# Weighted values with the values as weights: two groups' outputs in one PSUM bank, copied, turned back and added together

## What is computed

```python
ln_lat = layer_norm(latents, g2, b2); q = ln_lat @ Wq
kv = concatenate([layer_norm(x, g1, b1), ln_lat], axis=1) @ Wkv
k, v = split(kv, 2, axis=-1)                       # then 16 heads of 64
weight = einsum('bhld,bhnd->bhln', q * scale, k * scale)
weight = softmax(where(full_mask, weight, -max))   # full_mask: the mask, and all latents
out = einsum('bhln,bhnd->bhld', weight, v)         # then @ Wout, added to the latents
```

## Time and profile before

| | us |
|---|---|
| median of 3 runs | 1055.75 (1055.22 to 1056.27) |
| the profiled execution | 1054.65 |
| its span, first to last instruction | 1052.8 |
| TensorE busy in the span | 1014.3 |
| VectorE, ScalarE, GpSimd busy | 809.3, 666.8, 204.1 |
| cross stage, 30 to 660 us: TensorE, VectorE, ScalarE busy | 622.99, 485.98, 385.82 |

### The profile page before, as it was taken

How to read it: one execution, slowest core, us unless ns; L and a number is a source line. 1 busy time by engine, 2 the same in 40 slices (tenths; PEclk the granted TensorE clock), 3 DMA queues, 4 the chain that set the end, 5 groups by cost and what they waited for, 6 DMA issues and landing times. The chain is left out here.

```text
span 1052.8 us, 25657 instructions
## 1 busy us (share of the span) xinstructions
PE 1014.3 (96%) x8683; PEld 943.1 (90%) x8684; DVE 809.3 (77%) x3001; ACT 666.8 (63%) x1550; POOL 204.1 (19%) x265
## 2 busy tenths in 40 slices
PE   6999999999999999999999998988999999999997
PEld 6899999999999999999999998977888999889887
DVE  7887777685877786787787777579879889889753
ACT  4765565674665665566565566478776876767753
POOL 0111111110111111111111111342015203263213
PEclk9999999999999999999999999999999999999999
DMA  6000000000000000000000100520010000110000
GB/s 208 18 13 2 10 1 1 12 12 4 12 2 0 12 13 3 13 2 0 12 13 2 35 2 2 166 38 2 1 41 21 2 1 21 35 48 2 1 22 21
DMA packets 28803, 21.64 MB, mean 21 GB/s; under 512 B 12094, under 2 KB 26267, under 8 KB 28699
## 3 DMA queue, kind: packets, MB, share of 16 engines
q1 hardware_dynamic: 28529, 20.21, 6.5%
q10 hardware_dynamic: 170, 0.07, 0.0%
HBM read 19.17 MB, written 1.05 MB: 19 GB/s over the span
## 5 line engine op out<-in xcount | busy, mean ns | idle before, releaser
L303 PEld LDWEIGHTS pv_ps<-v,pt 128*128 128x128 f32 x1792 | 214.9, 192 | 9.3 <-issue 2.8
L303 PE MATMUL pv_ps<-v,pt 128*128 128x65 f32 x1792 | 215.2, 272 | 3.2 <-DVE o L818 1.8
L796 DVE CUSTOM_DVE_ANT_0 s_sb<-s_ps,pen,mstate 128x256 f32<-128x256 f32 (+1 forms) x512 | 199.9, 446 | 13.9 <-issue 11.0
L510 ACT ACTIVATE probs<-s_sb,mbias 128x256 f32<-128x256 f32 (+1 forms) x512 | 203.2, 470 | 0.0
L670 POOL TENSOR_TENSOR o<-o,alpha 128x260 f32<-128x260 f32 x128 | 85.7, 669 | 561.3 <-ACT alpha L504 561.3
L519 ACT ACTIVATE pt<-turn 128x512 f32<-128x512 f32 x128 | 76.2, 595 | 123.0 <-PE turn L290 109.1
L290 PE MATMUL turn<-ident,probs 128*128 128x128 f32 x896 | 123.8, 278 | 0.1
L290 PEld LDWEIGHTS turn<-ident,probs 128*128 128x128 f32 x896 | 98.8, 145 | 9.5 <-issue 0.3
L818 DVE TENSOR_TENSOR o<-o,pv_ps 128x260 f32<-128x260 f32 x128 | 53.9, 421 | 46.1 <-PE pv_ps L303 34.7
L279 PE MATMUL s_ps<-kh,qh 64*128 64x256 f32 (+1 forms) x512 | 78.9, 304 | 2.9 <-DVE x L840 1.6
L768 DVE TENSOR_TENSOR kl<-proj,kh 128x512 fp32r<-128x512 f32 (+1 forms) x63 | 41.3, 655 | 51.5 <-ACT kh L497 51.0
(11 more groups left out here) (432 smaller groups left out, 2730.7 us busy)
## 6 DMA issues: line engine op xcount, KB each, us to landing
raw<-in_ctx SPq DMA_DIRECT2D x24, 128.0 KB, 2.0
f_wqkv_raw<-in_L_ffn_wqkv SPq DMA_DIRECT2D x6, 512.0 KB, 5.3
f_w_raw<-in_L_ffn_w SPq DMA_DIRECT2D x8, 256.0 KB, 5.1
f_w_raw<-in_L_ffn_w SPq DMA_DIRECT2D x2, 640.0 KB
wkv_raw<-in_L_xattn_Wkv SPq DMA_DIRECT2D x1, 1024.0 KB, 8.5
wout_raw<-in_L_xattn_Wout SPq DMA_DIRECT2D x1, 1024.0 KB, 12.5
f_wo_raw<-in_L_ffn_wo SPq DMA_DIRECT2D x2, 512.0 KB, 4.7
x<-in_x SPq DMA_DIRECT2D x1, 768.0 KB, 9.6
```

The costliest lines, as they stand in the source:

```text
L303: last = pe.matmul(t.pv_ps[:, u, :], t.pt[g % 2][:, u, kt, :], t.v[:, kt, h, :], start=(kt == 0), stop=(kt == kts - 1))
L510: last = act.activation(t.probs[g % 2][:, u, 0:kts * P], t.s_sb[g % 2][:, u, 0:kts * P], ACT.Exp, bias=t.mbias[:, at:at + 1], scale=0.125)
L796: last = dve.tensor_tensor_reduce(out=t.s_sb[g % 2][:, u, 0:width], in0=t.s_ps[g % 2][:, u, 0:width], in1=t.pen[:, 0:width], scale=1.0, sc ...
```

## The change

The two operands of `weighted_values` change places. The weights are now 64 columns of `v` (one head, one key tile), and 256 columns of `pt` move (both query tiles of the head). The outputs come out turned: 64 partitions for each of the two heads of a group, 256 queries as columns. `pv_ps` is a bank of 2 x 256 columns, and two groups (`g` even and `g` odd) fill its two halves. In step `j` odd, for the pair that ends with group `j-4`: ScalarE copies the bank to SBUF at once (`store_outputs`, new tile `ov`), TensorE turns it back with four transposes into the same bank (`turn_back`, behind `turn_probs` and ahead of the projection), and VectorE adds all 512 columns to `o` (`add_outputs`, now behind `maxima` and `store_turned`). `weighted_values` waits on `o_added` only for even groups.

The column of ones goes. The sums of the weights come from the exponentials' accumulator (`accum_out`, new tile `sums`), and GpSimd adds them to the 65th column of `o` by a second instruction for each group, behind `p_ready`; `rescaled` counts two for each group.

Besides, two small tables of the opening (`key_row`, `below`) lie in `onorm`'s memory, and two semaphores of the opening are merged with others.

```diff
+    def pair_at(m, kind, prev, j):
+        return at_step(m, kind, prev, j - 4) if j % 2 else None
...
# TensorE
-                if g or not isinstance(m, int):
+                if g % 2 == 0 and (g or not isinstance(m, int)):
                     pe.wait_ge(s["o_added"], 8 * m + g)
-                for u in range(GU):
-                    h = 2 * g + u // QT
-                    for kt in range(kts):
-                        last = pe.matmul(t.pv_ps[:, u, :], t.pt[g % 2][:, u, kt, :], t.v[:, kt, h, :],
+                for kt in range(kts):
+                    for o, rows in enumerate((slice(0, DH), slice(DH, P))):
+                        last = pe.matmul(t.pv_ps[rows, g % 2, :], t.v[:, kt, 2 * g + o, :], t.pt[g % 2][:, QT * o:QT * o + QT, kt, :],
                                          start=(kt == 0), stop=(kt == kts - 1))
                 last.then_inc(s["pv_done"], 1)
+            def turn_back(m, g, kts):
+                pe.wait_ge(s["ov_stored"], 8 * m + g + 1)
+                for k in range(2):
+                    for qt in range(QT):
+                        last = pe.transpose(t.pv_ps[:, qt, k * P:(k + 1) * P], t.ov[:, k, qt * P:(qt + 1) * P], t.ident[:])
+                last.then_inc(s["o_turned_back"], 2)
...
                     if now:
                         turn_probs(*now)
+                    pair = pair_at(m, kind, prev, j)
+                    if pair:
+                        turn_back(*pair)
...
# ScalarE
-                                          bias=t.mbias[:, at:at + 1], scale=0.125)
+                                          bias=t.mbias[:, at:at + 1], scale=0.125, accum_out=t.sums[:, at:at + 1])
...
+            def store_outputs(m, g, kts):
+                act.wait_ge(s["pv_done"], 8 * m + g + 1)
+                if g >= 2 or not isinstance(m, int):
+                    act.wait_ge(s["o_turned_back"], 8 * m + g - 1)
+                act.activation(t.ov[:], t.pv_ps[:], ACT.Copy).then_inc(s["ov_stored"], 2)
...
                 for j in range(NG if kind else 6):
+                    pair = pair_at(m, kind, prev, j)
+                    if pair:
+                        store_outputs(*pair)
                     now = at_step(m, kind, prev, j - 2)
                     if now:
                         store_turned(*now)
...
# GpSimd
+                    pool.wait_ge(s["rescaled"], 16 * m + 2 * g + 1)
+                    pool.wait_ge(s["p_ready"], 8 * m + g + 1)
+                    pool.tensor_tensor(t.o[:, cols, DH], t.o[:, cols, DH], t.sums[:, cols], ALU.add).then_inc(s["rescaled"], 1)
...
# VectorE
-            def add_output(m, g, kts):
-                cols = slice(GU * g, GU * (g + 1))
-                dve.wait_ge(s["pv_done"], 8 * m + g + 1)
-                dve.wait_ge(s["rescaled"], 8 * m + g + 1)
-                dve.tensor_tensor(t.o[:, cols, :], t.o[:, cols, :], t.pv_ps[:], ALU.add).then_inc(s["o_added"], 1)
+            def add_outputs(m, g, kts):
+                cols = slice(GU * (g - 1), GU * (g + 1))
+                dve.wait_ge(s["o_turned_back"], 8 * m + g + 1)
+                dve.wait_ge(s["rescaled"], 16 * m + 2 * g + 1)
+                added = t.o[:, cols, 0:DH].rearrange("p (h q) d -> p h q d", q=QT)
+                dve.tensor_tensor(added, added, t.pv_ps[:].rearrange("p q (h d) -> p h q d", d=DH), ALU.add).then_inc(s["o_added"], 2)
...
-                    now = at_step(m, kind, prev, j - 4)
-                    if now:
-                        add_output(*now)
...
                     now = at_step(m, kind, prev, j - 2)
                     if now:
                         store_turned(*now)
+                    pair = pair_at(m, kind, prev, j)
+                    if pair:
+                        add_outputs(*pair)
...
-            t.v = sb("v", [P, KT, H, DH + 1])
+            t.v = sb("v", [P, KT, H, DH])
+            t.ov = sb("ov", [P, 2, L])
...
-            t.pv_ps = ctx.enter_context(nc.psum_tensor("pv_ps", [P, GU, DH + 1], F32))
+            t.pv_ps = ctx.enter_context(nc.psum_tensor("pv_ps", [P, 2, L], F32))
```

More of the change, by code:

```diff
@@ L109, in cross_stage @@
         "s_done", "s_read", "bias_ready", "alpha_ready", "p_ready", "t_done", "pt_ready",
-        "pv_done", "rescaled", "o_added", "inverse", "state_set",
+        "pv_done", "ov_stored", "o_turned_back", "rescaled", "o_added", "inverse", "state_set",
         "o_norm", "o_turned", "ot_stored", "ot_hi", "ot_lo", "out_done", "x_added",
         "ident_loaded", "keys_loaded", "first_x_loaded", "rest_loaded", "q_loaded", "k_loaded", "second_w_loaded", "third_w_loaded", "wv_loaded", "norm_turned",
-        "mask_loaded", "flags_ready", "flags_ranked", "keys_spread", "keys_listed",
+        "mask_loaded", "flags_ready", "flags_ranked",
         "w_hi", "w_lo", "plan_step", "plan_rows", "plan_moved", "plan_done")
@@ L159, in value_part @@
     def value_part(u):
-        return t.v[:, u % 2, (u // 2) * NG:(u // 2 + 1) * NG, 0:DH]
+        return t.v[:, u % 2, (u // 2) * NG:(u // 2 + 1) * NG, :]
     def load_norm(eng, which):
@@ L465, in _ @@
             project_keys(0, KB)
-            pe.wait_ge(s["keys_spread"], 1)
-            pe.matmul(t.pv_ps[0:B, 1, 0:NCH + 1], t.row_of[:], t.listed[:], start=True, stop=True).then_inc(s["keys_listed"], 1)
+            pe.wait_ge(s["flags_ready"], 3)
+            pe.matmul(t.pv_ps[0:B, 1, 0:NCH + 1], t.row_of[:], t.listed[:], start=True, stop=True).then_inc(s["flags_ranked"], 1)
             pe.wait_ge(s["w_lo"], 3)
@@ L502, in softmax_part @@
                 if not isinstance(m, int):
-                    act.wait_ge(s["rescaled"], 8 * m + g - 7)
+                    act.wait_ge(s["rescaled"], 16 * m + 2 * g - 14)
                 act.activation(t.alpha[:, GU * g:GU * (g + 1)], t.mdiff[:, GU * g:GU * (g + 1)], ACT.Exp,
@@ L679, in _ @@
             dve.memset(t.tick[:], 0.0).then_inc(s["s_read"], 2)
-            dve.memset(t.v[:, :, :, DH:DH + 1], 1.0).then_inc(s["x_added"], 2)
-            dve.memset(t.mask8[:, 1, :], 0)
+            dve.memset(t.mask8[:, 1, :], 0).then_inc(s["x_added"], 2)
             dve.memset(t.pen[:], 0.0).then_inc(s["pen_ready"], 1)
@@ L822, in normalise_output @@
                 dve.wait_ge(s["o_added"], 8 * m - 4 + 4 * half)
+                dve.wait_ge(s["rescaled"], 16 * m - 8 + 8 * half)
                 dve.reciprocal(t.inv[:, cols], t.o[:, cols, DH]).then_inc(s["inverse"], 1)
@@ L851, in body @@
                 for j in range(NG if kind else 6):
-                    now = at_step(m, kind, prev, j - 4)
-                    if now:
-                        add_output(*now)
-                    if finish and j in (0, 3):
-                        normalise_output(m, b, j // 3)
+                    if finish and j == 0:
+                        normalise_output(m, b, 0)
                     if kind and j == 4 and not final:
@@ L863, in body @@
                         store_turned(*now)
+                    pair = pair_at(m, kind, prev, j)
+                    if pair:
+                        add_outputs(*pair)
+                    if finish and j == 3:
+                        normalise_output(m, b, 1)
                     if finish and j in (1, 2, 4, 5):
@@ L950, in rank_flags @@
                 dve.tensor_scalar(t.listed[:, 0:NCH], t.key_row[:, 0:NCH], t.place[:], t.own_key[:], ALU.is_equal, ALU.mult
-                                  ).then_inc(s["keys_spread"], 1)
+                                  ).then_inc(s["flags_ready"], 1)
             twice, less = t.scratch[0:B, 0:ITEMS], t.scratch[0:B, ITEMS:ITEMS + NCH]
@@ L958, in plan_keys @@
                 dve.tensor_scalar(twice, t.iota[:], 2.0, None, ALU.mult)
-                dve.wait_ge(s["keys_listed"], 1)
+                dve.wait_ge(s["flags_ranked"], 2)
                 dve.tensor_copy(t.plan_rows[:, 0:NCH], t.pv_ps[0:B, 1, 0:NCH])
@@ L2548, in program @@
             t.mask_cols, t.listed, t.place = sb("mask_cols", [P, CH], U8), sb("listed", [P, NCH + 1]), sb("place", [P, 1])
-            t.key_row, t.key_col, t.own_key = sb("key_row", [P, P]), sb("key_col", [P, 1]), sb("own_key", [P, 1])
-            t.below, t.row_of = sb("below", [P, B, NCH]), sb("row_of", [P, B])
+            t.key_col, t.own_key = sb("key_col", [P, 1]), sb("own_key", [P, 1])
+            t.row_of = sb("row_of", [P, B])
             t.x_stats, t.x_mv = sb("x_stats", [P, TILES, 6]), sb("x_mv", [P, TILES, 2])
@@ L2566, in program @@
             t.pt = [sb(f"pt{k}", [P, GU, KT, P]) for k in range(2)]
-            t.mstate, t.mnew, t.mdiff, t.mbias, t.alpha, t.inv = (
-                sb(n, [P, H * QT]) for n in ("mstate", "mnew", "mdiff", "mbias", "alpha", "inv"))
+            t.mstate, t.mnew, t.mdiff, t.mbias, t.alpha, t.inv, t.sums = (
+                sb(n, [P, H * QT]) for n in ("mstate", "mnew", "mdiff", "mbias", "alpha", "inv", "sums"))
             t.o = sb("o", [P, H * QT, DH + 1])
             t.onorm = sb("onorm", [P, QT, H * DH])
+            t.key_row = t.onorm[:, 0, 0:P]
```

(1 more changed line is left out.)

## The result

The changed kernel takes 1140.3 us (median of 4 runs, 1139.6 to 1147.4; a fifth took 1136.0) beside 1055.5 us of the kernel before: a ratio of 1.081, 95% interval 1.0761 to 1.0858. It is slower by 84.8 us; the forecast was 77 slower, 1132 us, range 1106 to 1178. Its mean granted clock is 0.970, that of the other executions 0.975 to 0.980.

What follows compares the result with a forecast made beforehand. TensorE, busy 1014.3 of 1052.8 us, was taken to bound the kernel, its waits for other engines' answers deciding. Full pairs 39, half pairs 30 and VectorE 8 made +77 on 1054.65: 1132 us, range 1106 to 1178.

Steps and rivals of the forecast that it cites:

- The main term: Even step and turn back: TensorE waits for ScalarE's copy behind its exponentials, until P + 3.4; +1.27 us a full pair.
- 5 slots of 0.215: Full group's weighted values: 8 passes on two column halves overlap in order, lasting 1.08 us; bounds 0.86 and 1.72.
- the change of layout: TensorE's entry into the 64-column array layout: 0.2 us charged each time, bounds 0 and 0.3.
- the forecast -0.45: Odd step of a full pair: weighted values follow the turn back without a wait, 1.08 + 0.2 - 1.73 us.
- The 48 and 16 of the sum: Pairs counted over the kernel: 48 full pairs at +0.82 us, +39 us; 16 half pairs at 2.2 us, 35, taken as 30.
- the 30 us of the forecast: Half pairs: +1.8 us of waiting and +0.4 for the turn back, odd step 0; 16 x 2.2 = 35, taken as 30.
- The wait was forecast at 0.6 us in 13 items: Step 1 of an item: TensorE's next even group waits for VectorE's late addition, in about 13 of 16 items; +8 us.
- busy 21 of 30 at 1.00: TensorE's clock in the first 30 us, taken as ground that it stays at its upper level in spite of gaps.
- Column halves not side by side: Rival: weighted values' passes run one after the other, odd step +0.19 us; +111 us, 1166 us; chance 0.33.
- The turn back never waits: Rival: ScalarE's copy ends before TensorE's P + 2.2, so only TensorE's own work counts; -11 us, 1044 us; chance 0.05.

Runs made afterwards that it cites:

- even and odd pair of runs: Changed kernel with the weighted values' matmuls made twice, in even steps only: 1142.8 us; in odd steps only: 1187.4 us.
- early addition: Changed kernel with VectorE's addition moved between the second and third reduction of the odd step: 1125.8 us alone, 1043.0 us with ScalarE's copy moved too.
- the test: Changed kernel with ten needless transposes ahead of the turning back in half items and the first two pairs of the item behind them: 1129.8 us.
- early copy: Changed kernel with ScalarE's copy of the outputs moved behind the first of the even step's four exponentials: 1092.4 us alone.

## Why the prediction was right, step by step

**The main term held.** Even step and turning back were to cost +1.27 us a full pair. Measured from the end of the projection to the next one's start: 330.12 - 326.32 = 3.80 us, against 2.53 in the earlier trace rows, +1.27; the next pair gives 3.79. Inside it small errors cancel: the readouts and the copy came as worked out (0.095 each; 0.58 us less an overlap of 0.10), the turning back took 0.42 instead of 0.40. That the saved passes vanish in the wait is shown by the even and odd pair of runs. The two pairs measured are usual ones; not all 48 are, as the sum below shows.

**The passes.** I took 5 slots of 0.215, 1.08 us, on the ground that low and high passes of alternate heads overlap in order. It is 4 slots, 0.86 us, since each column half goes its own way: eight records more in the even step lengthen the group by 1.88 - 1.02 = 0.86 us. That one record of a matmul is the low and the other the high half of an fp32 number, as my 5 slots had it, no run shows; the trace shows two records for each matmul, and not what they carry. For the change of layout I charged 0.20 us. It is 0.09 ahead of the first record (326.41 - 326.20 instead of 0.12) and 1.02 - 0.86 = 0.16 from there to the next work; sixteen records show the same 0.16 over eight slots (327.84 - 325.96 - 1.72). Together that is 0.25 us; how much of it is the layout's no run separates. The odd step gains more than the forecast -0.45: from the projection's end to the next scores 332.73 - 331.63 = 1.10 us, where it was 308.71 - 306.88 = 1.83, -0.73. That step of the sum was mis-sized by 0.28 us, by the fifth slot and by the 0.10 us by which the scores came late before, which the 1.73 left out. A usual full pair costs +0.54, not +0.82, and 48 of them would be 26 us and not 39.

**All pairs.** The 48 and 16 of the sum are counted from the earlier trace rows: 128 copies of `pt` are 128 groups, two to a pair, and 1792 records are 16 for each of 96 full groups and 8 for each of 32 half ones. The timeline of the changed kernel shows the wait of each of the 64 pairs. The 48 full pairs waited 48.8 us in all, 1.02 on average, because around half items some wait only 0 to 0.8 us; the 16 half pairs waited 24.7 us, from 0.57 to 2.7 each. One half pair, and two full ones behind it:

```profile
246.96 0.65 PE L315 MATMUL pv_ps<-ident,ov 128*128 128x128 f32 x4 [2.68 <-ACT ov L533]
...
269.21 0.66 PE L315 MATMUL pv_ps<-ident,ov 128*128 128x128 f32 x4 [0.30 <-ACT ov L533]
282.49 0.60 PE L315 MATMUL pv_ps<-ident,ov 128*128 128x128 f32 x4
```

In the usual full pair the cost is the wait less 0.65 us (0.54 for 1.19). With that as an estimate for all, 48 cost some 17 us. In a half pair at a clock of 1.00, where TensorE's last work ahead of the weighted values ends at 228.95 us, the turning back starts at 231.91, 2.96 us later (3.0 was forecast), and the next projection at 232.32, 3.37 later, against 1.20 before: +2.17 for a wait of 1.62. The odd step saves 0.17 (0.58 and 0.09 against 0.84), where I took nothing. So a half pair costs its wait and 0.38 us, 16 of them some 31; the 30 us of the forecast hold.

**VectorE.** The wait was forecast at 0.6 us in 13 items, 8 us. In step 1 it is there:

```profile
342.80 1.08 PE L306 MATMUL pv_ps<-pt,v 128*64 128x256 f32 x8 [0.66 <-DVE o L845]
```

But it is there six times, 4 us. The other 12 of the 18 waits, 9.4 us of 13.4, from 0.15 to 1.8 us, stand mostly at half items and just behind them, where I charged nothing. That 13 is near 8 is partly luck. The early addition took 9 us of them away and gave 14.5.

**What was missing.** The clock: from the first 30 us, busy 21 of 30 at 1.00, I concluded that gaps don't lower it. In the cross stage it fell to 0.50 ten times all the same, at or behind waits most of which stand at half items; with those filled it fell four times, and the kernel took 10.5 us less. What makes it fall no run shows. The 5.4 us at the scores, for VectorE's results (1.6 before), were not in the sum either. So 17, 31, 12 (13.4 less the 1.8 of before) and 4 make +64, and the wait at `f_g` 2 (2.4 less 0.2). Of the measured 84.8 us some 19 are left. The clock is the only cause known for them: the test gave 10.5 back, and the falls lack 29 us in the profiled execution; that it is all of the 19 was not shown. The middle of the range held partly because errors have opposite signs: full pairs were taken too dear by some 22 us, and the clock was left out. (The 1132 itself is the profiled execution and 77; the median and 77 would be 1133.)

**The rivals.** "Column halves not side by side" was given 0.33 and 1166 us: made on purpose, in one run, it was 1171.5. That too is partly luck, since the clock was 0.993 there, where the sum for this rival, like the other, had no term for it. "The turn back never waits" was priced at 1044 us, decided by a chain shorter by 1.2 us: with the copy and the addition moved, the kernel took 1043.0. That the two figures are so near is partly chance: I had not seen that half of the way is VectorE's, without whose early addition the time is 1092.4.

## What to carry to other kernels

In this kernel the full engine hid the others only as long as it never asked them for an answer within the same step (512 readouts cost 1.6 us before, some 21 us in the changed kernel). When a change adds such a question, place the answer's whole chain (here copy, then addition) in the other engines' order before counting what the full engine saves. Taking away the wait that ends last shows the next one: the early copy alone gave back 48 us, some of it by the clock, and uncovered 34 us of a second wait, and only both together turned 8% slower into 1.3% faster. To learn whether an engine's work counts in a step, make it do that work twice there and see whether the end moves.

## What the runs showed of the hardware that was not expected

- On two column halves of the array the records of the fp32 matmuls started out of program order between the halves: four narrow records of the second head had started beside two wide ones of the first, and both loop orders gave 1.02 us for eight passes, where one column half alone took 1.87. What was said above of engines that execute in order held at the waits, not between these matmuls.
- Ten times in the cross stage the granted clock was 0.50 for 3 to 10 us, 58 us in all, at or behind waits of which one was 1.41 us, others 2.7 and 3.3; more work in the waits at half items made the kernel 10.5 us faster. Waits of 1.19 us in full pairs, at 326 to 341 us, and one of 1.62 us were followed by none.
- A readout of ScalarE's accumulator has a record of 190 ns, but puts the next instruction back by 0.095 us only (0.49 us from one exponential to the next, against 0.40 without).
